# Second norm turned by DMA in two rows ahead of head 7, two tiles each for residuals and turned first norm, next graph's queries and keys earlier

## The reference

```
h = maximum(layernorm(x), 0)
q, k, v = heads(h @ Wq + bq), heads(h @ Wk + bk), heads(h @ Wv + bv)     # 16 heads of 32
attn = softmax(where(adj == 0, -inf, q @ k.T / sqrt(32)))
x = x + (attn @ v) @ Wo + bo
h = maximum(layernorm(x), 0)
alpha = maximum((h @ wq1) @ (h @ wk1).T, 0) * (adj != 0)
x = x + softmax(alpha, axis=1) @ (h @ weight)
```

## Time and profile before

| | before |
|---|---|
| median of 3 runs | 1569.95 us (1569.84 to 1571.14) |
| profiled execution, its own time | 1570.8 us |
| its span, first to last instruction | 1569.0 us |
| PE busy | 1504.6 us, 96% of the span |
| DVE, ACT, POOL busy | 80%, 72%, 68% |
| mean granted TensorE clock | 0.992 |

### The profile page before, as it was taken

The page is one execution under the profiler, slowest core; times in us unless marked ns, Lnnn a source line. Parts: engine busy times, 40 slices in busy tenths (PEclk is TensorE's granted clock), DMA queues, the critical chain, the costliest instruction groups (busy, mean ns, idle before and its releaser), DMA issues.

```text
span 1569.0 us, 50846 instructions
## 1 busy us (share of the span) xinstructions
PE 1504.6 (96%) x16561; PEld 1106.7 (71%) x16561; DVE 1247.9 (80%) x4042; ACT 1128.3 (72%) x2477; POOL 1064.8 (68%) x1478
## 2 busy tenths in 40 slices
PE   2889999999999999999999999999999999999996
PEld 1557777777777777777777777777777777777753
DVE  6778888887887878788888878888887888888763
ACT  2567777777777777777777777777777777777761
POOL 2466767777677777767677776777776777777650
PEclk9999999999999999999999999999999999999998
DMA  7647777667667766666776766777676677767760
GB/s 241 135 95 132 133 163 160 152 136 152 138 138 166 160 144 143 144 136 148 166 157 141 152 140 134 154 160 159 135 158 136 133 161 160 153 135 159 125 119 16
DMA packets 656198, 226.28 MB, mean 144 GB/s; under 512 B 611488, under 2 KB 627872, under 8 KB 656160
## 3 DMA queue, kind: packets, MB, share of 16 engines
q1 hardware_dynamic: 636848, 188.57, 59.1%
q10 hardware_dynamic: 19312, 37.23, 8.5%
HBM read 57.94 MB, written 16.78 MB: 48 GB/s over the span
## 4 chain that ended last, share of the span: by engine, by line
POOL 35%; issue 34%; PE 22%; DVE 4%; ACT 2%; DMA 1%; POOLq 1%; SPq 0%; ACTq 0%; DVEq 0%
PE ring L408 18%; POOL wv_raw L1115 16%; POOL heads_out L1149 6%; POOL x L1172 4%; POOL keep L1181 3%; POOL far L1190 3%; POOL xa L1137 1%; PE score L464 1%; PE pv L483 1%; DMA turned<-wv_raw 1%; POOL newton L1133 1%; PE ring L518 1%; PE pv L485 0%; DVE wk_raw L864 0%; DVE tops L785 0%
## 5 line engine op out<-in xcount | busy, mean ns | idle before, releaser
L1115 POOL TENSOR_TENSOR wv_raw<-wk_raw,wv_raw 128x512 f16<-128x512 f32 x512 | 608.0, 1190 | 362.8 <-ACT wv_raw L638 358.5
L625 ACT ACTIVATE wk_raw<-wk_raw,least 128x256 f32<-128x256 f32 x1024 | 459.0, 497 | 6.8 <-DVE least L864 6.8
L864 DVE CUSTOM_DVE_ANT_0 wk_raw<-score,far,undo_score 128x256 f32<-128x256 f32 x1024 | 444.0, 478 | 7.1 <-issue 5.1
L638 ACT ACTIVATE wv_raw<-wk_raw 128x512 f16<-128x512 f32 x512 | 320.5, 626 | 8.6 <-issue 4.5
L483 PEld LDWEIGHTS pv<-val,turned 128*128 128x128 f16 x2048 | 149.7, 97 | 67.4 <-issue 43.9
L483 PE MATMUL pv<-val,turned 128*128 128x65 f16 x2048 | 185.9, 192 | 10.8 <-DMA turned<-wv_raw 7.0
L408 PE MATMUL ring<-wv_hi,h 128*128 128x256 f16 x1024 | 189.3, 273 | 0.0
L408 PE MATMUL ring<-h,wq_hi 128*128 128x256 f16 x1024 | 176.3, 274 | 7.6 <-DVE wk_lo L827 7.6
L1149 POOL TENSOR_TENSOR heads_out<-o_sum,o_rcp 128x64 f32<-128x64 f32 x512 | 153.0, 320 | 42.6 <-DVE o_sum L879 42.6
L485 PE MATMUL pv<-val,turned 128*128 128x33 f16 x2048 | 178.1, 179 | 0.0
L408 PE MATMUL ring<-h,wk_hi 128*128 128x256 f16 x1024 | 176.6, 274 | 0.0
(11 more groups left out here) (151 smaller groups left out, 3570.6 us busy)
## 6 DMA issues: line engine op xcount, KB each, us to landing
xin<-x_dram ACTq DMA_DIRECT2D x32, 512.0 KB, 3.8
out_dram<-xo SPq DMA_DIRECT2D x32, 512.0 KB, 3.7
xa<-x_dram ACTq DMA_DIRECT2D x31, 512.0 KB, 4.2
adj_in<-adj_dram SPq DMA_DIRECT2D x32, 256.0 KB, 2.9
turned<-wv_raw SPq DMA_TRANSPOSE x512, 3.2
adjt_in<-adj_t_dram SPq DMA_DIRECT2D x32, 256.0 KB, 3.1
wq_raw<-wq_dram SPq DMA_DIRECT2D x2, 512.0 KB, 7.0
wk_raw<-wk_dram SPq DMA_DIRECT2D x2, 512.0 KB, 8.6
```

What stands on the lines that cost most here:

```text
L625: last = nc.scalar.activation(probs[:, at, q, :], probs[:, at, q, :], ACT.Exp, bias=least[:, at, q:q + 1], scale=-1.0)
L638: nc.scalar.activation(halves[:, at, :, 0, :], probs[:, at, :, :], ACT.Copy).then_inc(hi["p"], 1)
L864: last = nc.vector.tensor_tensor_reduce(out=probs[:, at, q, :], in0=score[u % GROUP][:, q * NODES:(q + 1) * NODES], in1=far[:, q, :], scal ...
L1115: nc.gpsimd.tensor_tensor(halves[:, at, :, 1, :], probs[:, at, :, :], halves[:, at, :, 0, :], ALU.subtract).then_inc(lo["p"], 1)
```

## The change

- The pieces `h2_0` and `h2_1` are gone. ACT and DVE now write the two halves of the second norm from `work` into a tile `half2` (`second_half`, in step 4, ahead of the evacuation of `qk3`), and SP turns them by two DMAs into `h2` in step 5 (`TURN2_STEP`, `transpose_h2`), ahead of the turn of head 7.
- The turned first norm `h1` has two tiles, one for even and one for odd graphs. Its two turns are issued in steps 3 and 5 (`TURN1_STEPS`) and no longer in step 6. `qk0` and `qk1` of the next graph, which read it, stand in steps 6 to 8 and no longer in steps 9, 10 and 13.
- The residual has two tiles as well, in place of `x1` and `xo`; `av1` moves into step 0 of the following body, `av0` to step 15, and the store from step 1 to step 9. `g`, `hw` and `al` move later by up to two steps, `hw1` from step 12 to 13; the softmax parts go from step 12 to 13.
- `g` and `hw` share memory with the raw `wk1_t`.
- At the start: the first norm of graph 0 is normalised on DVE and no longer on POOL, the weights `wk` are loaded on ACT's queue, the first products wait for two and no longer four split weights, the scale of the merged weights is found in two batches, and eight small matmuls are added. At the end, the last two bodies have tables of their own (`DENSE_LAST`, `DENSE_END`).

```diff
 DENSE = [
-    ["qk2a"],
+    ["av1", "qk2a"],
     ["wo0a", "ot1", "qk2b"],
     ["wo0b", "wo1a"],
     ["wo1b"],
     ["qk3"],
-    ["v1a", "h2_0", "h2_1", "v1b"],
-    ["g0"],
-    ["g1a"],
+    ["v1"],
+    ["qk0a", "qk0b"],
+    ["qk1a"],
+    ["qk1b", "g0a"],
+    ["g0b", "g1a"],
     ["g1b", "hw0a"],
-    ["hw0b", "qk0a"],
-    ["qk0b", "ala"],
-    ["alb", "ot0"],
+    ["hw0b", "ot0"],
+    ["al"],
     ["hw1"],
-    ["qk1"],
-    ["v0a", "av0"],
-    ["av1", "v0b"],
+    ["v0a", "v0b"],
+    ["av0"],
 ]
...
-HIGH1_STEP, LOW1_STEPS, TURN1_STEP = 14, (0, 2), 6
-VAR2 = 4
+HIGH1_STEP, LOW1_STEPS, TURN1_STEPS = 15, (0, 2), (3, 5)
+VAR2, TURN2_STEP = 4, 5
...
+            def transpose_h2(q, b):
                 if started(b - 1):
+                    sp.wait_ge(mm["hw"], count(b - 1, 2, 1))
                     settle(sp, sp_settled)
+                    sp.wait_ge(mm["al"], count(b - 1, 1, 0))
+                    settle(sp, sp_settled)
+                sp.wait_ge(lo["h2"], count(b, QT, q))
+                settle(sp, sp_settled)
+                sp.dma_start_transpose(
+                    h2[:, :, :, q * P:(q + 1) * P].rearrange("p h d n -> p (h d) n"),
+                    half2[:, q, :, :].rearrange("p h d -> p (h d)")).then_inc(h2_in, 16)
...
                     if head:
                         transpose_probs(*head)
-                    if s == TURN1_STEP and nxt:
-                        transpose_h1(n)
+                    if s in TURN1_STEPS and nxt:
+                        transpose_h1(TURN1_STEPS.index(s), n, 1 - odd)
+                    if s == TURN2_STEP and prev:
+                        for q in range(QT):
+                            transpose_h2(q, p)
...
-                if name.startswith("h2"):
-                    pe.wait_ge(normed[1], count(b, 2, k))
-                    for d in range(KT):
-                        last = nc.tensor.transpose(dst[:, d * P:(d + 1) * P],
-                                                   work[:, k, d * P:(d + 1) * P], ident[:])
-                    last.then_inc(mm["h2"], 1)
...
+            def second_half(q, b):
+                act.wait_ge(normed[1], count(b, QT, q))
+                if started(b - 1):
+                    act.wait_ge(h2_in, count(b - 1, QT, QT - 1) * 16)
+                nc.scalar.activation(half2[:, q, 0, :], work[:, q, :], ACT.Relu
+                                     ).then_inc(hi["h2"], 1)
```

More of the change, by code:

```diff
@@ L113, in started, with deal, order @@
     return not (isinstance(graph, int) and graph < 0)
+def deal(t):
+    if isinstance(t, int) and t >= BATCH - 1:
+        return DENSE_LAST if t == BATCH - 1 else DENSE_END
+    return DENSE
 def bank_before(name, t):
-    at, shift = ORDER.index(name), 0
+    def order(body):
+        return [other for step in deal(body) for other in step if not other.endswith("b")]
+    body, at = t, order(t).index(name)
     while True:
@@ L121, in bank_before @@
         if at < 0:
-            at, shift = at + len(ORDER), shift - 1
-        other = ORDER[at]
+            body -= 1
+            at = len(order(body)) - 1
+        other = order(body)[at]
+        graph = body + ROLE[other]
         if BANK[tile(other)] != BANK[tile(name)]:
             continue
-        graph = t + shift + ROLE[other]
-        if t + shift == 0 and tile(other) in SPARE:
+        if body == 0 and tile(other) in SPARE:
             return other, -1 - t
-        if t + shift < -1:
+        if body < -1:
             return None, 0
@@ L236, in two_layers @@
         stored = sem("stored")
[L237 removed]
+        h1_in, h2_in = sem("h1_in"), sem("h2_in")
         small_in = sem("small_in")
@@ L337, in _ @@
             sp.dma_start(xa[:], x_v[0, :, :, :]).then_inc(xa_in, 16)
+            for half in range(2):
+                load_raw(sp, "wq", half)
             sp.dma_start(bias_q[:], bq).then_inc(small_in, 16)
@@ L444, in merge @@
                                                 stop=(k == KT - 1))
-                else:
-                    for half in range(2):
-                        wait_raw(pe, "wo", half)
-                    for k in range(KT):
-                        last = nc.tensor.matmul(dst[:], bv_wide[:, k, :], raw["wo"][:, k, :],
-                                                start=(k == 0), stop=(k == KT - 1))
                 last.then_inc(merged, 1)
@@ L596, in body @@
                         spread_scale(0, 2, pv)
-                    if nxt and not cur and s == step_of("qk0") - 1:
+                        for _ in range(WARM):
+                            nc.tensor.matmul(ring[1][:, 0:P], ident[:], ident[:], start=True,
+                                             stop=True)
+                    if nxt and not cur and s == step_of("qk0"):
                         turn_tops(1, pv)
-                    if nxt and not cur and s == step_of("qk0"):
-                        spread_scale(1, 1, pv)
                     if s in SCORE_STEPS:
@@ L766, in body @@
                         act.dma_start(xa[:], x_v[n + 1, :, :, :]).then_inc(xa_in, 16)
+            for half in range(2):
+                load_raw(act, "wk", half)
             act.wait_ge(const_ok, 2)
```

379 lines of the change are left out of this document (223 added, 156 removed).

## The result

The changed kernel takes 1840.45 us, median of 4 runs (1836.59 to 1845.57), against 1570.55 of the kernel before in the same series: 1.172 times as long, 95% interval 1.168 to 1.176. I had forecast 1617 and a range that ended at 1640. The direction was right, the size was not: 270 us instead of 47.

The account below looks back on a forecast made before the run. PE was taken as the bound, full in the steady graphs. Three waits over 30 bodies add 87 us, less 34.4 for transposes and 6 at the start: +46.6, about 1617 us (3% slower), range 1595 to 1640.

Parts of the forecast that it names:

- The gain of 1.11 us per graph: The second norm's eight transposes leave PE: 1.11 us per graph, 34.4 us over the 31 graphs where PE is the bound.
- First term: PE waits at qk0 in step 6 for the first norm's second turned half: 1.4 us per graph.
- Second term: PE waits at weigh(7) for head 7's turn, delayed by a load in the queue: 0.6 us per graph.
- Third term: PE waits before av0 for the softmax's hw_lo on DVE: 0.9 us per graph.
- fourth rival: The queue congests, all terms at their upper ends or beyond: over 1640 us; chance 0.07.
- Start and end: Earlier normalisation and qk0 starting on wq alone save 6 us at the start (3 to 9); the end changes by 0.
- What the profile would show: Gaps on PE before qk0, weigh(7) and av0, each ended by its supplier; period near 47.8 us; PE busy about 94%.

Follow-up runs that it names:

- h2: g2 with the residual's input load moved from step 4 to 13, the store from 9 to 14, the next-but-one input's load from 7 to 8: 1609.8 us.
- f1: The kernel before with its loop over graphs written out, nothing else changed: 1588.8 us.
- i2: h3 with the residual's input load at step 10, the store at 11, the adjacency loads in steps 12 and 13 of the body before: 1596.8 us.
- f4: Changed kernel written out, step 13's masks behind the softmax, exponentials at steps 11 and 12, first norm's turns at 1 and 3, load at 7: 1691.1 us.
- g0: The changed kernel written out, with the sum of pair 6 moved before e_lo on DVE: 1764.1 us.
- g2: f4 with the sum of pair 6 before e_lo as well, the masks of step 13 behind hw_lo: 1647.9 us.
- h3: h2 with the first of step 13's two masks before e_lo and the second behind hw_lo: 1602.6 us.
- h4: g2 with only the two masks split, one before e_lo and one behind: 1632.3 us.
- e2_unrolled: The changed kernel with its loop of two bodies replaced by all bodies written out: 1710.2 us.
- f2_softmax: The changed kernel written out, with step 13's masks behind the softmax and the first transposed exponentials at steps 11 and 12: 1744.2 us.
- after: The changed kernel itself, two bodies to a pass of its loop, against the kernel before: 1840.45 us.
- e1_before_two: The kernel before with two bodies in a pass of its loop in place of one, nothing else: 1668.7 us.

## Why the prediction was right in direction and wrong in size

**The step that failed is one that I left out.** My account of the change went through what it adds and moves within a body, and the diff has a line on the loop itself: since the two tiles of `h1` and of the residual alternate, a pass now holds two bodies. I gave it no price and did not name it. It costs 130 us of the 270: 1840.5 less 1710.2. The page before had a sign of it, 0.48 MB of instructions for 50,846 executed ones; I had not read those rows.

**The gain of 1.11 us per graph shows in part.** PE is busy for 1150.08 of 1200 us in h2's stretch from 300 to 1500 us, with 47.1 us from graph to graph: 45.2. In f1 it is 1239.83 of 1260, with 46.6: 45.9. The difference is 0.7 us of the 1.11, and PE's busy times are modelled.

**First term, 1.4 us at `qk0` (0.8 to 1.9).** Right in place and cause, somewhat short in size; written out it is 75.2 less the 9 at the start, 66 over 31 graphs, 2.1 us. In the loop it is 5.4 us in some graphs, 1.6 in others. The bank of `qk3`, which I had put inside this term, shows once the turn is early: 0.5 us in 19 graphs of i2.

**Second term, 0.6 us at head 7 (0 to 1.0).** Right in place and near in the mean: written out, PE waits there for 25.0 us, 0.8 per graph. But it is 17 graphs with up to 2.75 us and none in the others, where I had one value for all. I had put it down to the load at the end of step 5. No run moves this load alone: in f4, which moves it together with the turns, 10.3 us are left at head 7, and head 8, next to the load's new place, waits 22.5. That plain transfers do this is shown by h2, where head 8 no longer waits.

**Third term, 0.9 us before `av0` (0.3 to 1.2).** Wrong in place and short in size: it stands before `weigh(14)`, 1.6 us in each steady graph (with the ends, 46.7 us over the 28 graphs, 1.7). I followed the softmax to `hw_lo` and asked who waits for that; I did not ask what is queued behind it on DVE. The wait that I had forecast lies hidden behind this one: with the sum out of the way (g0) `av0` waits 2.0 us for `hw_lo`, some 1.0 of it because `e_lo` met POOL.

**With the terms as measured.** From head 0 of graph 3 to that of graph 31 the kernel written out takes 1416.95 us, 129.8 more than before. PE's waits in it are 60.5 us at `qk0`, 46.7 for the sum and 29.8 for turned halves: 137.0 where there were 1.9, 4.8 us more per graph where I had 2.9. PE's busy time there is 1279.80 us against 1285.23, 5.4 us less and not 31. The clock is a good part of the difference: it is granted at 0.50 for 51.2 us of the stretch, which costs at most 25.6 us (i2, with hardly any of this, is 18 us less busy than the kernel before over the same graphs). Start and end take 11 us more, not 6 less. Together this is the 141 us between the two spans (1709.8 and 1569.0); some 14 us of the waits come with the straight line itself (f1). My fourth rival (all terms at or above their ends, over 1640 us) was the nearest and had 0.07.

**The clock was in no term.** I added waits as if each cost its own length. In the changed kernel PE's busy time is 51.5 us above that of the same bodies written out.

**The start did not give 6 us.** In i2 head 0 of graph 3 is weighed at 203.3 us, against 199.36, and from that of graph 31 on it takes 82.9 us where it took 82.5. Which of the edits at the start failed is not shown.

**What the profile would show.** PE's gaps before `qk0` and `weigh(7)` came as said, the one before `av0` did not, and two stood where I had not looked: `weigh(14)` and the start of a pass. The period is about 50 and about 60 us by turns, 54.9 in the mean, not 47.8.

**What stays open.** Of the 59 us between g2 (1647.9) and f1 (1588.8), 38 were plain transfers (h2) and 7 to 16 the order of DVE's queue (h3, h4). In i2 PE still waits 28.0 us for turned halves, 10.7 for the staging of queries and keys ahead of `qk0`, 9.2 for `o_sum` and 5.1 at the scores. In the 28 graphs from head 0 of graph 3 on, PE is busy for 1267.12 of 1304.26 us in i2 and for 1284.27 of 1305.33 in f1: what the change saves on PE (17 us) goes into waits (16). I removed none of them alone. Why a straight line alone brings the turned halves' waits from 7.0 to 21.4 is not separated, nor is why four bodies to a pass bring them to 62.1.

## What to carry to other kernels

When a change alternates two buffers in a loop over blocks, price the longer pass before the buffers: compare the bytes on the instruction queues with the instructions executed. If far fewer were read than run, the body is being kept, and doubling it can cost more than any wait that it removes (here 98 us on a kernel with nothing else changed). On an in-order engine ask of a moved piece both who waits for it and who is queued behind it. And read the granted clock behind each wait on PE: some of the waits here cost their length twice.

## What the runs showed of the hardware that I had not expected

- The idle time of 1.63 us at `weigh(14)` was followed by the full clock in 28 of 28 graphs (e2_unrolled). Around the end of one of 2.21 us the granted clock fell to 0.50 in 10 of 29 graphs (f2_softmax) and in 15 of 29 (f4_all), for 3.4 us each; behind 0.26 and 2.04 us with eight small products between it fell in 14 of 28 (g0_sum_ahead). With the 13 pauses of 3.0 to 5.5 us it was at 0.50 until 2.8 to 6.0 us behind their end (after).
- Two engines on one port pair can lock into a phase: `e_lo` met POOL in 28 of 32 graphs of the looped form (1.42 us for its second tile) and in one of the written-out form (0.48 in the others).
- A loop's body of about 1,035 matmuls and weight loads on PE is read once and kept (0.48 MB of instructions in the whole run); with two in a pass each instruction is read as often as it runs, and each pass but the first starts with a pause of 3.4 to 4.5 us (e1_before_two).
- A turned half with no other transfer in flight lands 3.1 us after its issue begins (the median in g2_all_sum, 200 to 1450 us), and 4.4 us with a plain load or store in flight at some time before it lands, a tenth of them over 5.8. Moving three such transfers is worth 38 us (h2_loads).
